# First transfers and mask stores reordered, and the background work of four batch groups redistributed over the heads of a fused macaron kernel

## The reference

```python
x = x + 0.5 * ffn(layernorm(x), weight, bias)
x = x + attn(layernorm(x), Wq, bq, Wk, bk, Wv, bv, Wo, bo, phase, threshold, temperature)
x = x + 0.5 * ffn(layernorm(x), weight, bias)

# ffn: activations and weight in blocks of 32, each block scaled to at most 7.5 and
# rounded to the nearest value of a 6-bit float grid, scaled back, then out = xd @ wd.T + bias
# attn: scores = Q K^T / sqrt(8) + 0.3 * log(mask + 1e-6), softmax over the keys, times V, then @ Wo + bo
# mask[h] = sigmoid((sin(pq)cos(pk) + sin(pk)cos(pz) + sin(pz)cos(pq) - t) / (temperature + 1e-6)),
#   one 512 x 512 mask per head, the same for all sequences, from position and phase[h]
```

## Time and profile before

| what | us |
|---|---|
| median of three runs | 913.27 (909.49 to 916.39) |
| the profiled execution, its own time | 915.71 |
| its span, first to last instruction | 913.7 |
| first score product of head 0 | at 143.76 |
| first exponential of q1, q2, q3 | at 325.31, 513.99, 700.87 |
| mean granted TensorE clock | 0.942 |

### The profile page before, as it was taken

The page is one execution under the profiler, slowest core; times in us unless marked ns, Lnnn a source line. Parts: engine busy times, 40 slices in busy tenths (PEclk is TensorE's granted clock), DMA queues, the critical chain, the costliest instruction groups (busy, mean ns, idle before and its releaser), DMA issues.

```text
span 913.7 us, 12885 instructions
## 1 busy us (share of the span) xinstructions
PE 729.2 (80%) x4355; PEld 257.3 (28%) x4355; DVE 532.2 (58%) x1308; ACT 672.3 (74%) x795; POOL 187.4 (21%) x164
## 2 busy tenths in 40 slices
PE   0367606899898888999879889999889888998944
PEld 0043300242222222433323224333233122322334
DVE  8776752764553376756784586567943323465264
ACT  1388734888787888888867888887768878888811
POOL 0306731103333110032252020133630000020011
PEclk9987755999999999999999999999999999999986
DMA  5639595643777674537776655477666655554201
GB/s 149 118 123 363 194 374 182 225 152 110 206 224 223 190 201 154 159 107 202 225 201 214 190 172 169 129 205 204 190 187 213 184 163 165 168 181 151 80 1 50
DMA packets 56068, 162.10 MB, mean 177 GB/s; under 512 B 14120, under 2 KB 24496, under 8 KB 45578
## 3 DMA queue, kind: packets, MB, share of 16 engines
q1 hardware_dynamic: 51740, 154.36, 55.1%
q0 software_dynamic: 1808, 5.94, 2.1%
q10 hardware_dynamic: 2446, 0.89, 0.6%
HBM read 117.87 MB, written 43.29 MB: 176 GB/s over the span
## 4 chain that ended last, share of the span: by engine, by line
PE 49%; DVE 15%; DMA 11%; ACT 11%; issue 9%; SPq 3%; POOL 1%; DVEq 0%; POOLq 0%; ACTq 0%
PE S_PS L1512 20%; PE O_PS L1526 17%; DVE S_PS L1148 8%; ACT BIG L682 7%; DMA BIG<-shift_rows 5%; PE F_PS L1417 3%; PE R_PS L1535 3%; DMA PART<-trig_parts 2%; ACT BIG L728 1%; DMA k_parts<-PART 1%; PE F_PS L1412 1%; SPq L331 1%; PE P_PS L1417 1%; SPq L334 1%; DMA q_parts<-PART 1%
## 5 line engine op out<-in xcount | busy, mean ns | idle before, releaser
L682 ACT ACTIVATE BIG<-S_PS 128x1024 f32<-128x1024 f32 x512 | 508.9, 1024 | 151.3 <-PE S_PS L1512 149.9
L1512 PE MATMUL S_PS<-BIG 98*128 98x512 bf16 x1024 | 303.9, 390 | 83.3 <-DVE S_PS L1148 47.0
L1526 PE MATMUL O_PS<-BIG,VX 128*9 128x512 f32 x2048 | 270.4, 601 | 0.9 <-issue 0.9
L1148 DVE COPY S_PS<-BIG 128x1024 f32<-128x1024 f32 x128 | 152.1, 1224 | 159.1 <-ACT BIG L682 157.5
L1512 PEld LDWEIGHTS S_PS<-BIG 98*128 98x128 bf16 x1024 | 74.6, 98 | 345.8 <-ACT BIG L682 128.8
L1161 DVE RECIPROCAL RD<-R_PS 128x16 f32<-128x16 f32 x64 | 16.4, 257 | 124.6 <-PE R_PS L1535 124.1
L533 POOL TENSOR_TENSOR XDT<-PART 128x512 bf16<-128x512 f32 x24 | 26.7, 1111 | 252.0 <-ACT PART L650 252.0
L1526 PEld LDWEIGHTS O_PS<-BIG,VX 128*9 128x9 f32 x2048 | 30.8, 88 | 112.2 <-issue 97.7
L510 POOL TENSOR_TENSOR BIG<-BIG,BFH 128x512 f32<-128x512 f32 x16 | 21.9, 1398 | 186.9 <-DVE BIG L980 134.5
L510 POOL TENSOR_TENSOR X<-X,BFH 128x512 f32<-128x512 f32 x16 | 26.0, 1652 | 151.0 <-DVE BIG L980 76.0
L542 POOL TENSOR_TENSOR PART<-PART 128x512 f32<-128x512 f32 x32 | 37.1, 1161 | 69.7 <-DVE PART L1051 68.5
(11 more groups left out here) (190 smaller groups left out, 743.0 us busy)
## 6 DMA issues: line engine op xcount, KB each, us to landing
BIG<-ln_masks SPq DMA_DIRECT2D x62, 1024.0 KB, 6.3
ln_masks<-BIG SPq DMA_DIRECT2D x16, 1024.0 KB, 7.5
BIG<-q_parts SPq DMA_DIRECT2D x63, 192.0 KB
BIG<-k_parts SPq DMA_DIRECT2D x63, 144.0 KB
BIG<-q_parts SPq DMA_DIRECT2D x63, 128.0 KB
q_parts<-PART SPq DMA_DIRECT2D x9, 768.0 KB, 3.8
k_parts<-PART SPq DMA_DIRECT2D x18, 384.0 KB, 4.5
BIG<-k_parts SPq DMA_DIRECT2D x63, 96.0 KB
```

The costliest lines, as they stand in the source:

```text
L682: act.activation(E[:, m % 2, j, 2 * pair:2 * pair + 2, :], S_PS[:, pair, :, :], ACT.Exp, scale=LOG_WEIGHT)\
L1148: ve.tensor_copy(S_PS[:, pair, :, :], LNM[:, slot, 2 * pair:2 * pair + 2, :]).then_inc(s["seeded"], 1)
L1512: mm = pe.matmul(S_PS[:, pair, i, :], KT[0:ALL_ROWS, slot, K_COL[j], 128 * kb:128 * kb + 128], QT[0:ALL_ROWS, slot, j, :], start=False, st ...
L1526: mm = pe.matmul(O_PS[32 * j:32 * j + HD + 1, :], VX[:, slot_of(n), j, kb, h, :], E[:, m % 2, j, kb, :], start=kb == 0, stop=kb == T - 1)
```

## The change

It does the following.

- **Masks and first transfers.** SP waits for the first half's trig functions before it loads QM of the second half and the further copies. Seven masks instead of eight are stored before `load_x(1)`; masks 0 and 8 follow, then the loads of the stack and shift rows of head 1, then SP waits for all of head 0's stack; only then are masks 9 to 12 stored, masks 13 and 14 in `head(1)`, 15 in `head(2)`. `load_x(3)` and `load_x(2)` move from `head(0)` and `head(1)` to `head(2)` and `head(3)`.
- **TensorE before the heads.** Group 0's first chain steps, its norms included, stand ahead of the third `val` of the second half; the others stand with up to two `val`s between, the last four with none.
- **Background.** FIRST is carried out in q0 alone, for group 1. The first feed-forward of groups 2 and 3 is done a quarter earlier, in q0 and q1, in two halves of two sequences (LATE), with F_PS and XDT[1] alone. The chains start at ticks 8, 40, 72 and 96 in q1 and q2, and as before in q0; their `norm` moves to four ticks ahead of each chain. LAST runs from tick 24 to 91 instead of 50 to 127. SP's and GpSimd's orders follow, and outputs are stored at heads 11 to 14.

The diff, cut to its core (ScalarE's, VectorE's and TensorE's tick loops follow the tables in the same way):

```diff
-CHAIN = (48, 64, 80, 96)
-SECOND = dict(turn_pe=0, xnt_act=1, q_pe=4, q_act=5, k_pe=8, k_act=9, v_pe=12, v_ve=13, hi_q_ve=8, mid_q_ve=10,
-              hi_k_ve=11, mid_k_ve=13, norms_k_pe=14, k_top_ve=16, norms_q_pe=18, sq_ve=19, sqrt_act=21,
+
+LATE = ((dict(stats_ve=(52, 53), lnexp_act=55, rstd_ve=60, centre_ve=65, reduce_ve=66, scales_ve=68, to_grid_ve=73,
+              from_grid_ve=76, turn_pe=(80, 85), xd_copy_act=(81, 86), ffn_pe=(82, 87), add_ve=(84, 89),
+              lnexp1_act=91, rstd1_ve=92),
+         dict(stats_ve=(81, 82), lnexp_act=84, rstd_ve=94, centre_ve=97, reduce_ve=98, scales_ve=100, to_grid_ve=105,
+              from_grid_ve=108, turn_pe=(110, 115), xd_copy_act=(111, 116), ffn_pe=(112, 117), add_ve=(113, 118),
+              lnexp1_act=121, rstd1_ve=123)),
+        (dict(stats_ve=(42, 44), lnexp_act=46, rstd_ve=49, centre_ve=74, reduce_ve=75, scales_ve=80, to_grid_ve=81,
+              from_grid_ve=82, turn_pe=(93, 98), xd_copy_act=(94, 99), ffn_pe=(95, 100), add_ve=(97, 102),
+              lnexp1_act=104, rstd1_ve=107),
+         dict(stats_ve=(89, 90), lnexp_act=92, rstd_ve=96, centre_ve=99, reduce_ve=100, scales_ve=105, to_grid_ve=106,
+              from_grid_ve=108, turn_pe=(112, 117), xd_copy_act=(113, 118), ffn_pe=(114, 119), add_ve=(115, 120),
+              lnexp1_act=122, rstd1_ve=124)))
+
+CHAINS = ((48, 64, 80, 96), (8, 40, 72, 96), (8, 40, 72, 96), ())
+SECOND = dict(norm_ve=-4, turn_pe=0, xnt_act=1, q_pe=4, q_act=5, k_pe=8, k_act=9, v_pe=12, v_ve=13, hi_q_ve=8,
+              mid_q_ve=10, hi_k_ve=11, mid_k_ve=13, norms_k_pe=14, k_top_ve=16, norms_q_pe=18, sq_ve=19, sqrt_act=21,
               row_ve=24, turn_bound_pe=26, bound_act=27)
 
-LAST = dict(turn_pe=(50, 58, 66, 74), at_act=(51, 59, 67, 75), out_pe=(54, 62, 70, 78), add_ve=(57, 65, 73, 81),
-            centre_ve=83, lnexp_act=84, rstd_ve=88, reduce_ve=89, scales_ve=92, to_grid_ve=96, from_grid_ve=99,
-            turn_xd_pe=(104, 110, 116, 122), xd_copy_act=(105, 111, 117, 123), ffn_pe=(108, 114, 120, 126),
-            add_ffn_ve=(109, 115, 121, 127))
+LAST = dict(turn_pe=(24, 32, 40, 48), at_act=(25, 33, 41, 49), out_pe=(26, 34, 42, 50), add_ve=(27, 35, 43, 51),
+            centre_ve=52, lnexp_act=53, rstd_ve=56, reduce_ve=57, scales_ve=60, to_grid_ve=64, from_grid_ve=67,
+            turn_xd_pe=(73, 77, 81, 88), xd_copy_act=(74, 78, 82, 89), ffn_pe=(75, 79, 83, 90),
+            add_ffn_ve=(76, 80, 84, 91))
...
         def calls_of(n, k):
-            return 2 if k == 1 or (k == 2 and n == NQ - 1) else 1
+            halved = {0: range(2, NQ), 1: range(2 * NQ), 2: range(NQ - 1, NQ)}
+            return 2 if n in halved[k] else 1
...
         def first_bank(n, j):
-            return (P_PS, F_PS)[j % 2]
+            return F_PS if n in (2, 3) else (P_PS, F_PS)[j % 2]
+
+        def first_turned(n, j):
+            return XDT[1] if n in (2, 3) else XDT[j % 2]
...
-                if more:
-                    if m + 1 >= 2:
-                        load_mask(m + 1)
+                if more and m >= 1:
+                    load_mask(m + 1)
+                    if m == 1:
+                        for h in range(13, 15):
+                            store_mask(h)
                     load_stack(sp, m + 1)
                     if i < NH - 1:
                         load_shift(sp, m + 1)
-                if m == 0:
+                if m == 2:
+                    store_mask(15)
                     sp.wait_ge(s["val_ready"], 2 * HALF_TILES)
                     load_x(3)
-                if m == 1:
+                if m == 3:
                     lnm_stored(sp, 15)
                     load_x(2)
-                if q > 0 and i in (13, 14, 15):
-                    store(q - 1, i - 13)
-                if q > 1 and i == 0:
-                    store(q - 2, 3)
-                if q < NQ - 1:
-                    if i in (9, 11, 13, 15):
-                        store_shift(q + 1, (i - 9) // 2)
-                    if i in (7, 9, 11, 13):
-                        store_q(sp, q + 1, (i - 7) // 2)
-                        store_k(sp, q + 1, (i - 7) // 2)
+                if q > 0 and i in (11, 12, 13, 14):
+                    store(q - 1, i - 11)
+                for j, c in enumerate(CHAINS[q]):
+                    if i == (c + SECOND["bound_act"]) // STEPS:
+                        store_shift(q + 1, j)
+                    if i == (c + SECOND["norms_k_pe"]) // STEPS:
+                        store_q(sp, q + 1, j)
+                        store_k(sp, q + 1, j)
                 if more and i == NH - 1:
...
             load_functions(QM, 0, 0, 0, "trig_in")
+
+            sp.wait_ge(s["trig_in0"], 96)
             load_functions(QM, 0, 1, 0, "trig_in")
             sp.wait_ge(s["trig_out_k"], 16)
             for half in range(2):
@@ -472,15 +495,20 @@
                     load_functions(QM, 0, half, copy, "trig_more")
                     load_functions(KM, 1, half, copy, "trig_more")
 
-            for h in MASK_ORDER[0:8]:
+            for h in MASK_ORDER[0:7]:
                 store_mask(h)
             lnm_stored(sp, 3)
             load_x(1)
-            for h in range(8, 16):
+            store_mask(0)
+            store_mask(8)
+
+            load_stack(sp, 1)
+            load_shift(sp, 1)
+            sp.wait_ge(s["first_stack"], K_LOADS)
+            for h in range(9, 13):
                 store_mask(h)
             for m in range(NQ * NH):
                 head(m)
-            store(NQ - 2, 3)
...
-            def bias_before(n):
-                pool.wait_ge(s["quant0"], n * K_QUANT + 1)
-                for j in range(QB):
+            def bias_before(n, js=range(QB)):
+                for j in js:
+                    pool.wait_ge(s["quant0"], (calls_before(n, 0) + j * calls_of(n, 0) // QB) * K_QUANT + 1)
                     add_bias(x_of(n)[:, j, :, :], BFH, "xa_biased")
...
+            def batch(n, j):
+                chain(n, j)
+                start_after(n, j)
+
+            bias_before(1)
+            batch(1, 0)
+            batch(1, 1)
+            bias_before(2, range(0, 2))
+            batch(1, 2)
+            batch(1, 3)
+            bias_before(2, range(2, 4))
+            batch(2, 0)
+            batch(2, 1)
+            bias_after(0)
+            batch(2, 2)
+            bias_before(3, range(0, 2))
+            batch(2, 3)
+            bias_before(3, range(2, 4))
+            batch(3, 0)
+            batch(3, 1)
+            bias_after(1)
+            batch(3, 2)
+            batch(3, 3)
+            bias_after(2)
             bias_after(NQ - 1)
...
+                if n in (2, 3):
+
+                    act.wait_ge(s["ffn_psum0"], n * QB + j)
+                    if j == 0:
...
                 if f == 0 and past(n):
-                    ve.wait_ge(s["xn_turned"], QB * n)
+                    ve.wait_ge(s["xn_turned"], QB * (n - 1) + js.stop)
...
+                    for j, c in enumerate(CHAINS[q]):
+                        n = q + 1
+                        if q > 0 and tick == c + SECOND["norm_ve"]:
+                            norm(n, j)
...
             def turn_xd0(n, j):
-                pe.wait_ge(s["quant0"], (n + 1) * K_QUANT)
-                if j >= 2:
+                pe.wait_ge(s["quant0"], (calls_before(n, 0) + j * calls_of(n, 0) // QB + 1) * K_QUANT)
+                if n in (2, 3):
+                    pe.wait_ge(s["ffn_added0"], n * QB + j)
+                    if j == 0:
...
-            turn_xn(0, 0)
-            project_q(0, 0)
-            turn_xn(0, 1)
-            project_k(0, 0)
-            project_v(0, 0)
-            steps = [(project_q, 1), (turn_xn, 2), (norms_k, 0), (norms_q, 0), (project_k, 1), (project_v, 1),
-                     (project_q, 2), (turn_xn, 3), (norms_k, 1), (norms_q, 1), (project_k, 2), (project_v, 2),
-                     (project_q, 3), (norms_k, 2), (norms_q, 2), (project_k, 3), (project_v, 3)]
-            for t in range(HALF_TILES + 2, 2 * HALF_TILES):
-                val(t)
-                what, j = steps[t - HALF_TILES - 2]
+            for what, j in ((turn_xn, 0), (project_q, 0), (turn_xn, 1), (project_k, 0), (project_v, 0), (project_q, 1)):
+                what(0, j)
+            norms_k(0, 0, 0)
+            norms_q(0, 0)
+
+            steps = [(2, turn_xn, 2), (2, project_k, 1), (2, project_v, 1), (2, norms_k, 1), (0, norms_q, 1),
+                     (2, project_q, 2), (1, turn_xn, 3), (1, project_k, 2), (1, project_v, 2), (1, norms_k, 2),
+                     (0, norms_q, 2), (0, project_q, 3), (0, project_k, 3), (0, project_v, 3)]
+            t = HALF_TILES + 2
+            for tiles, what, j in steps:
+                for _ in range(tiles):
+                    val(t)
+                    t = t + 1
                 if what is norms_k:
                     norms_k(0, j, 0)
                 else:
                     what(0, j)
-            for what, j in steps[HALF_TILES - 2:]:
-                what(0, j)
```

(1 more changed line is left out.)

214 lines of the change are left out of this document (116 added, 98 removed).

## The result

The kernel after takes 943.18 us (median of four runs, 936.83 to 945.38) where the kernel before took 913.53 beside it (909.49 to 916.39): a ratio of 1.033, 95% interval 1.029 to 1.038. The profiled execution took 941.33 with a span of 939.4. I had forecast 904: the sign was wrong.

What follows compares the result with a forecast made beforehand. Heads bound by ScalarE plus 1.5 or TensorE plus 0.4, or store-to-score transfers; setup's end by a transfer chain. First score -12.5, masks +2.5, quarters +1.5 make -8.5 on 915.7: 907.2, median 904.8, forecast 904; own range 898 to 909, cases 893 to 913.

Steps and rivals of the forecast that it cites:

- q0, +6: First quarter of the heads: gains group 2's first feed-forward, head 10 +2.0, head 14 +1.4; +6 us in all.
- q1 and q2, -4.5: Second and third quarters: lose the store head where VectorE was full, giving 187 and 184 us; -4.5 us together.
- Levelling pays: Rival over the quarters: they save 8 us rather than lose 1.5, total 895 us; chance 0.18.
- q3, 0: Last quarter of the heads: same work done earlier, no change in time.
- The K store, -7.8: End of setup: the last sequence's K parts land in 4.9 us instead of 12.71 without masks beside them; -7.8 us.
- The masks weren't the cause: Rival at end of setup: K store or shift store stays as long, half the gain goes, 911 us; chance 0.25.
- The shift rows, -3.2: End of setup: the shift rows' store waits 4.0 us instead of 7.17, between bounds 7.17 and 2.1; -3.2 us.
- The chains, -2.0: Group 0's chains before the heads: one mask fewer ahead of the first Q store, gain reaching the last K store; -2.0 us.
- the order of TensorE "at nothing": Before the heads: moving chain steps ahead of `val`s costs nothing, or up to 2 us if the masks' sigmoids starve.
- The trig gate, +0.5: Setup: further copies go out later behind one more transfer's landing; 0.5 us lost, bounds 0.85 gained and 4.8 lost.
- The masks, +2.5: Heads 1 and 2: masks 9 to 14 delay head 1 by 1.9 us, head 2 nothing or a microsecond; +2.5 us.
- the backlog rival: Heads 1 and 2: 7.3 MB ahead of head 2's stack go at 200 GB/s, not 395; 922 us, chance 0.10.

Runs made afterwards that it cites:

- all places mended: Kernel after with old transfers, gate and TensorE order, LAST and LATE pairs in ticks 2, 3, 6, 1, large VectorE entries out of tick 6: 935.52 us, 1.021.
- the tables: Only the change's new background tables, with the kernel before's transfers, trig gate and TensorE order ahead of the heads: 942.05 us, 1.0325.
- the run with both edits: Change's division of work with pairs in ticks 2, 3, 6, 1, plus new transfers with stack and shift-rows loads ahead of mask stores: 924.85 us, 1.0105.
- the stack first: Kernel before's tables and TensorE order, change's transfers and gate, next head's loads ahead of mask stores, mask 15, x3, x2 later: 905.78 us, 0.989.

## Why the prediction was wrong

**The step that failed.** "I add a turn and product as 1.34 of TensorE and 0.64 of ScalarE", and "VectorE is free up to some 9 us": I priced work by the engine's total in a head. The 0.64 was read from q3 head 7 of the kernel before, whose pair stands in ticks 2 and 6, and I gave it to pairs in ticks 0 and 2, which cost 1.24, though the diff showed the new ticks. VectorE's limit was read as a total too; the costly heads have 5.93 to 13.97 us of VectorE, q0's heads 15 and 12 no more than 5.93 and 9.06, and stall because other work stands between the seeds or ahead of a bound. The larger part is the term "The operations are the same save for halves": I gave the move of the first feed-forward out of empty heads into full ones +6 in q0 and nothing in q1, which I even made shorter. With all places mended it costs 10.4 in q0 and 11.3 in q1 (below).

**q0, +6.** Heads 10 and 14, which I had priced with their feed-forward (+2.0 and +1.4), grew by 1.5 and 0.85. Heads 12 and 15, which I gave nothing and about 0.5, grew by 2.7 and 3.8, both with a wait for the second seed. Heads 6 to 15 took 10.6 more.

**q1 and q2, -4.5.** They took 12.7 more. One benefit that I forecast came in q2, whose head 12 fell from 14.69 to 11.19, but q1 paid 12.2 for LATE. I had counted the first feed-forward as the same work wherever it went; it went from empty heads (at most 3.0 us) to full ones. That is the levelling itself: against the kernel before on the same chip the tables cost 29.4 us (942.05 and 912.68) and with all places mended still 20.5 (935.52 and 915.06), all of them in q0 and q1, where LATE stands. "Levelling pays" (895) failed with it.

**q3, 0.** It took 2.7 more, for five heads of one pair in the dear ticks and two with more work (12.30 and 11.83). In the good ticks it took 163.3 in the run with both edits, 2.4 less than before, of which 1.6 are a head that fell to a clock of 0.85 in the kernel before (11.57 for 9.96).

**The K store, -7.8.** Right, and larger: 9.1; the 4.9 had been read behind a Q store twice as large. "The masks weren't the cause" fell. The store takes 3.61 us behind its Q store alone and took 12.71 beside mask stores, 3.5 times as long (10.9 to 12.7 in the eight profiles with the old transfers). The queues of the kernel before, from the Q store's first packet on (122.2 to 128.6): packets, MB, share of the engines.

```profile
q1 hardware_dynamic: 234, 1.74, 69.3%
q0 software_dynamic: 218, 0.79, 32.6%
```

q1 is SP's queue with the masks, q0 GpSimd's with the Q and K stores. In these 6.4 us GpSimd's queue sent nearly as many packets as SP's, 218 and 234, but SP's were twice as large (7.4 KB in the mean against 3.6), so of the 2.53 MB GpSimd's queue moved 0.79, a third. And 4.6 of the 12.71 us lie before the first packet, which came 5.3 us after the Q store's issue at 116.95 and 1.3 after it in the kernel after; what it waited for there was not separated.

**The shift rows, -3.2.** 1.0. With no mask in flight their store took 6.21 and, with the stack first, 6.46; the bound of 7.17 was nearly the value, and my "between them" had no row.

**The chains, -2.0, with the order of TensorE "at nothing".** The store moved by +2.0. With the old transfers it went out at 116.6 to 119.7 in eight profiles, 117.75 in the mean, and with the new ones and TensorE's order of before at 117.0 in the mean of four: the transfers gave 0.7, within the scatter, where I took 2.0. The order cost some 2.3; it had no bound in my sum beyond "up to 2 us".

**The trig gate, +0.5.** It wasn't run by itself. The products that waited 0.85 us began at 43.17 in the kernel after and at 43.80 and 42.82 in the two runs with the transfers and the old tables, around the 43.64 of before: no loss of 0.5 is seen.

**The masks, +2.5.** The first half of the step was right: four mask stores landed 12.5 us after their issue, forecast 12.9, and head 1 stalled. The second failed: "mask 2's load and masks 13 and 14 (3.1 MB, 8.0 us) stand ahead of head 2's stack, which lands near 155". It landed at 161.7. With the tables of before, heads 0 to 5 cost 8.5 more and not 2.5. It wasn't the slow rate of the backlog rival, 200 GB/s (up to that landing the queue moved 343), but the order: with the stack first the heads took 63.75 us. What decides is what the small transfer that is wanted next stands behind.

**Left open.** How much of the 12 to 14 us of LATE is the low clock was not separated. By an estimate from rows it is the smaller part: one stretch at half clock (0.50) made a bare head of 9.96 last 11.57 (q3 head 3, kernel before), and q1 has two such stretches more than q2, some 3 us. Why full heads pay the rest, where mended ticks don't help, is not shown.
